# Half-position selective scans taken by pairs of states, with the side products of a lane moved

## The chip, the cores and the metric

The program runs on one core of one Trainium2 chip. The metric is the device time of one execution in microseconds. Each core has TensorE (PE, with its weight loads PEld), VectorE (DVE), ScalarE (ACT), GpSimd (POOL) and SyncE (SP, which here issues the DMAs); each of them works through its own instructions in order, and they meet at semaphores.

## The reference

Four images of 384 x 32 x 32 go through two layers. Layer 0: a scan in four directions (K0 = 4, 384 channels, 16 states) and a small FFN. Layer 1: a Mamba block (768 channels, 16 states) and a mixture of 4 experts. What the change touches is the recurrence, for each channel, direction and state n:

```
dA = exp(dt * A[n])
h  = h * dA + (dt * u) * B[n]
y += h * C[n]          # summed over the 16 states
```

with `dt = softplus(...)`, B and C rows shared by all channels of a direction. After it come the skip product, gates, output projections and norms.

## The kernel before

Channels lie on the 128 partitions, positions (1024 per image) on the free axis. The first image and its Mamba block take whole rows of 1024 (`lane_scans`, before 1237 us); the other three images and Mamba blocks take half rows of 512 (`fused_scans`), which is what the change touches. The program calls it three times for images (24 lanes each: 4 directions x 2 halves x 3 channel tiles) and three times for Mamba (12 lanes: 2 halves x 6 tiles). Lanes go half by half: the first half of a direction starts from zero and its last states are kept in `carry`, the second half starts from them.

A lane is 16 steps, one for each state. ACT's `decay(s)` writes exp(dt A) into a PSUM bank (L1297). POOL's `drive(s)` multiplies du by the B row (L1400, ring of DRIVES = 3). DVE's `scan(s)` runs the recurrence (L1449) and writes h over the decay, or into a `held` buffer where `by_pool(s)` holds. `weigh(s)` multiplies h by the C row: on DVE into `prods` for 11 states of a lane (L1458), on POOL in place in `held` for 5 (L1410). PE's `add(s)` sums over the states in bank 0 by four transposing matmuls (L1157). ACT copies that sum (`copy_sum`, L1321, step 3 of the next lane), PE turns it back (`back`, L1201), and a `take` on DVE (images) or `take_skipped` on ACT (Mamba) brings it to its place. In first halves, ACT's `keep` (L1289) and a POOL copy (L1408) save the last state before its bank or buffer is reused.

For the next lane, PE makes the dt product (L1141), ACT takes abs, exp and ln of it (L1277, L1281, L1285), DVE makes delta (L1430) and POOL du (L1389).

The order of each engine is written out by hand, by the constants `..._AT`: at which step of a lane an engine does what. Banks 1 to 4 of PSUM are a ring (SLOTS = 4): the list `places` names who takes the next one, steps and, between them, the projection of the next direction, delta, sum, output, gate input and residual. Whoever takes a place waits in `vacated` for the occupant four places earlier: a step weighed on DVE frees its bank with its weighing (and keep), one held for POOL with its scan.

Into this are woven guests: the expert products of the image before (`up`, `gelu`, `down` on banks 5 to 7). The gelus, a pair at a time with a table load ahead and one behind (L1341, L1379), stand behind the decay of steps 8, 13 and 18 (= 2 of the next lane) in images, 8 and 16 (= 0) in Mamba. Mamba lanes 0, 1, 2, 5, 6, 7 make a gate besides, with a silu and two table loads on ACT; lanes 8 to 10 an output product, lane 4 a projection; image lanes 0 to 7 turn a residual tile, lanes 1, 4, 7, 10, 13, 16, 19 project. In image lanes 0 to 2 ACT turns the image (L1363) at step 14.

## Time and profile before

| | |
|---|---|
| median of three runs | 5609.17 us (5603.15 to 5609.78) |
| the profiled execution's own time | 5607.85 us |
| its span | 5606.0 us, 73119 instructions, mean granted clock 0.945 |
| busy over the span | PE 86%, DVE 79%, POOL 71%, ACT 65% |
| half scans of images | about 1237 to 1930, 2555 to 3240, 3866 to 4550 us |
| half scans of Mamba | about 2100 to 2460, 3410 to 3760, 4700 to 5080 us |

Busy time is counted per engine. A wait is put down to the semaphore that came last. In a time line the difference of two starts on one engine is what an instruction costs its engine; it can be a little less than its length, since one overlaps the next.

### The profile page before, as it was taken

Reading aid. Unit: us, or ns where it says so; the run is one execution under the profiler, and the core shown is the slowest. Engines: PE = TensorE matmul, PEld = TensorE weight load, DVE = VectorE, ACT = ScalarE, POOL = GpSimd, SP = SyncE. Lnnn points to the kernel's source line nnn. Section 1 sums busy time; section 2 is a strip of 40 time slices with the busy share of each in tenths; the row PEclk is TensorE's granted clock in tenths of the full one; section 3 lists DMA queues with packets and bytes.
Section 4 is the critical chain, followed back from the end, with each engine's and each line's share of the span. In section 5 each row is a group of like instructions: output and inputs, shape, how many; then the busy total and the mean of one; then the engine's idle time right before and its main releaser. Section 6 shows DMA issues by size and latency. Waiting matters only on the chain. (4 is left out here: it accounts for less than half of the span.)

```text
span 5606.0 us, 73119 instructions
## 1 busy us (share of the span) xinstructions
PE 4828.6 (86%) x23205; PEld 3411.3 (61%) x23205; DVE 4445.6 (79%) x4529; ACT 3634.0 (65%) x5725; POOL 3960.4 (71%) x3074
## 2 busy tenths in 40 slices
PE   7888797789898887888989888888998988888998
PEld 5776546656666645555666645565666654556777
DVE  6889838959999848977999957996999975896544
ACT  5666455448887757767878857775878865775222
POOL 5888619839999818857999935894999962984111
PEclk9999999989999998998999999998999999999999
DMA  5777607737877616647788724654877842562110
GB/s 206 263 252 264 211 10 258 252 132 254 287 268 268 226 34 219 224 135 250 260 280 271 269 69 171 220 183 161 281 266 276 271 166 102 201 216 93 43 43 29
DMA packets 356676, 1104.83 MB, mean 197 GB/s; under 512 B 33210, under 2 KB 121126, under 8 KB 354872
## 3 DMA queue, kind: packets, MB, share of 16 engines
q1 hardware_dynamic: 356280, 1100.06, 56.9%
q8 instruction: 187, 3.06, 0.2%
q14 instruction: 209, 1.71, 0.1%
HBM read 1086.24 MB, written 13.68 MB: 196 GB/s over the span
## 5 line engine op out<-in xcount | busy, mean ns | idle before, releaser
L1157 PE MATMUL banks<-ident,prod 128*128 128x128 f32 x4752 | 764.9, 287 | 392.5 <-DVE prod L1458 286.6
L1157 PEld LDWEIGHTS banks<-ident,prod 128*128 128x128 f32 x4752 | 556.8, 145 | 799.1 <-DVE prod L1458 557.8
L1449 DVE TENSOR_TENSOR_SCAN banks<-banks,h 128x512 f32<-128x512 f32 x594 | 723.3, 1218 | 85.8 <-ACT banks L1297 48.5
L1400 POOL TENSOR_TENSOR h<-lane,Bb 128x512 f32<-128x512 f32 x576 | 722.8, 1272 | 57.8 <-DMA Bb<-half_rows 33.8
L1297 ACT ACTIVATE banks<-lane,A 128x512 f32<-128x512 f32 x864 | 581.1, 686 | 251.6 <-DVE prod L1458 82.4
L1229 PE MATMUL banks<-w_a,Cb 128*128 128x384 f32 x1536 | 552.2, 488 | 0.0
L1449 DVE TENSOR_TENSOR_SCAN banks<-banks,half_carry_a,h 128x512 f32<-128x512 f32 x396 | 505.5, 1277 | 8.8 <-ACT banks L1297 4.9
L1400 POOL TENSOR_TENSOR h<-half_du_a,Bb 128x512 f32<-128x512 f32 x384 | 482.7, 1275 | 14.8 <-DMA Bb<-half_rows 10.1
L1297 ACT ACTIVATE banks<-half_delta_a,A 128x512 f32<-128x512 f32 x576 | 385.3, 685 | 151.5 <-DVE lane L1430 73.7
L1217 PE MATMUL banks<-big,w_a 128*128 128x256 f32 x1728 | 435.0, 394 | 1.0 <-DMA w_a<-w_in 0.8
L1458 DVE TENSOR_TENSOR prod<-banks,half_C_a 128x512 f32<-128x512 f32 x528 | 365.3, 692 | 73.4 <-DMA half_C_a<-half_rows 2.4
L506 PE MATMUL banks<-diagonals_first,Cb 128*128 128x128 f32 x2304 | 318.1, 296 | 90.2 <-DVE h L771 39.0
L1400 POOL TENSOR_TENSOR h<-lane,Cb 128x512 f32<-128x512 f32 x288 | 362.7, 1272 | 24.8 <-DVE banks L1449 14.9
L659 ACT ACTIVATE banks<-delta_first,A 128x1024 f32<-128x1024 f32 x144 | 160.7, 1116 | 333.0 <-DVE prod L778 243.9
L506 PEld LDWEIGHTS banks<-diagonals_first,Cb 128*128 128x128 f32 x2304 | 299.7, 209 | 123.9 <-issue 120.4
L1341 ACT ACT_TABLE_LOAD x288 | 369.5, 1283 | 7.1 <-PE banks L1229 1.9
L1379 ACT ACT_TABLE_LOAD x288 | 369.5, 1283 | 5.2
L1217 PEld LDWEIGHTS banks<-big,w_a 128*128 128x128 f32 x1728 | 325.7, 198 | 61.7 <-issue 11.6
L1229 PEld LDWEIGHTS banks<-w_a,Cb 128*128 128x128 f32 x1536 | 269.7, 191 | 127.2 <-issue 12.0
L2436 POOL TENSOR_TENSOR w_lo<-raw,w_hi 128x1152 fp32r<-128x1152 f32 x32 | 89.3, 2812 | 352.8 <-ACT w_hi L2516 352.7
L1410 POOL TENSOR_TENSOR h<-h,half_C_a 128x512 f32<-128x512 f32 x240 | 305.0, 1271 | 46.6 <-DVE h L1449 36.0
L1157 PE MATMUL banks<-ident,h 128*128 128x128 f32 x2160 | 334.3, 279 | 0.0
(471 smaller groups left out, 12291.6 us busy)
## 6 DMA issues: line engine op xcount, KB each, us to landing
Bb<-half_rows SPq DMA_DIRECT2D x576, 512.0 KB, 4.3
C_first<-rows SPq DMA_DIRECT2D x288, 512.0 KB, 5.4
Cb<-half_rows SPq DMA_DIRECT2D x288, 512.0 KB, 4.4
w_a<-w_in SPq DMA_DIRECT2D x256, 576.0 KB, 6.1
w_b<-w_in SPq DMA_DIRECT2D x128, 576.0 KB, 6.2
half_C_a<-half_rows SPq DMA_DIRECT2D x128, 512.0 KB, 6.7
Bb<-rows SPq DMA_DIRECT2D x96, 512.0 KB, 5.5
half_C_b<-half_rows SPq DMA_DIRECT2D x64, 512.0 KB, 6.6
```

What stands on the lines that cost most here:

```text
L506: mm = eng.matmul(in_bank(2 + 2 * (s % SLOTS), k), m.du_turned[i % 2][:, block_of(k)], diagonal(n)[:, block_of(k)], start=k % (HALF // P) ...
L659: eng.activation(to, m.delta[:, i % 2, :], ACT.Exp, scale=lanes[i].A[:, a:a + 1]).then_inc(st.decay, 1)
L1157: mm = eng.matmul(ps[:, 0, at], src[:, at], m.ident[:, :], start=n == 0 and k == 0, stop=added(s) == (i + 1) * N, is_transpose=True, skip_ ...
L1217: mm = eng.matmul(hidden(u), g.w1[:, w % WRING, k, t * P:(t + 1) * P], g.un[:, k, at], start=k == 0, stop=k == CT - 1, skip_group_check=True)
L1229: mm = eng.matmul(total(b), g.h[:, u % HRING, b * P:(b + 1) * P], g.w2[:, w % WRING, t, :], start=u % PER == 0, stop=u % PER == PER - 1, s ...
L1297: eng.activation(slot(s), m.delta[i % 2], ACT.Exp, scale=x.A(j, n)).then_inc(st.decay, 1)
L1341: eng.activation(g.h[:, u % HRING, :], hidden(u), ACT.Gelu, bias=m.vec[:, b:b + 1]).then_inc(st.gelu, 1)
L1379: eng.preload_act_table_set(EXP_LN)
L1400: eng.tensor_tensor(m.dBu[:, s % DRIVES, :], m.du[i % 2], m.B[b % BRING][:, cols(s % 2)], ALU.mult).then_inc(st.dbu, 1)
L1410: eng.tensor_tensor(h, h, m.C[:, s % N, :], ALU.mult).then_inc(st.pooled, 1)
L1449: eng.tensor_tensor_scan(flip(to), flip(slot(s)), flip(m.dBu[:, s % DRIVES, :]), initial, ALU.mult, ALU.add).then_inc(st.scanned, 1)
L1458: eng.tensor_tensor(prods[own(s) % PRODS], slot(s), m.C[:, n, :], ALU.mult).then_inc(st.prod, 1)
```

## The change

Drives, weighings and keeps go by pairs of states (1024 wide instead of 512, one instruction where there were two); scans and decays stay one for each state. Of the eight pairs of a lane, 0, 3 and 5 are weighed on POOL and the others on DVE (6 and 10 states, where it was 5 and 11). The rings are of pairs: two drives, two products, two held (one of them in new SBUF). The bank ring keeps its four banks, but a pair takes two neighbouring ones, so that `places` is filled up with `None` behind or ahead of a lone side product; `vacated` skips a `None` to the occupant before it. Projection, residual, gate input and output product stand ahead of step 14, are made by PE at steps 12 and 13 and copied by ACT at step 15. The dt product goes from step 0 behind the add to step 1, ahead of adds; abs, exp, ln stand behind decay 4 (before: behind decay 5); du goes from step 14 to ahead of the drive of pair 4. PE makes adds after the side products of a step. POOL runs one drive ahead and weighs a pair after the drive of the second next. The two late silu inputs move to `prod[:, 2]`, and `turned_sum` too.

```diff
+def late_input(m, f):
+    return m.prod[:, CT - 1, cols(LATE_SILUS.index(f))]
...
-    SLOTS, DRIVES, PRODS, HELD, BRING = 4, 3, 3, 3, 3
+    SLOTS, DRIVES, PRODS, HELD, BRING = 4, 2, 2, 2, 3
-    PROJECT_AT, LOW_AT, STORE_AT = 11, 13, 15
-    COPY_AT, BACK_AT, TAKE_AT, SUM_AT, DELTA_AT = 3, 4, 7, 8, 4
-    SKIP_TAKE_AT = 9
-    BEHIND = 2
-    GATE_AT, PRODUCT_AT, OUT_AT, OUT_COPY_AT = 9, 6, 9, 11
+    ALL_PAIRS = LANES * PAIRS
+    POOLED, DU_AT, BEHIND = (0, 3, 5), 3, 2
+    DELTA_PLACE_AT, SUM_PLACE_AT, OTHER_PLACE_AT = 4, 8, 14
+    DT_AT, MAGNITUDE_AT, DELTA_AT = 1, 4, 5
+    COPY_AT, BACK_AT, TAKE_AT, SKIP_TAKE_AT, GATE_AT = 3, 6, 8, 9, 10
+    PROJECT_AT, LOW_AT, STORE_AT = 12, 15, 15
+    PRODUCT_AT, OUT_COPY_AT = 12, 15
-    INPUT_AT, INPUT_PLACE_AT, INPUT_TAKE_AT = 6, 9, 11
+    INPUT_AT, INPUT_TAKE_AT = 12, 15
-    TURN_AT, TURN_PLACE_AT, TURN_TAKE_AT = 11, 14, 15
+    TURN_AT, TURN_TAKE_AT = 12, 15
...
-        return s % N % 3 == 1
...
+    def by_pool(b):
+        return b % PAIRS in POOLED
...
-        if fresh(step // N + 2) and step % N == PROJECT_AT:
-            places.append(("projection", step // N + 2))
-        if step // N + 1 < LANES and step % N == DELTA_AT:
-            places.append(("delta", step // N + 1))
-        if step // N and step % N == SUM_AT:
-            places.append(("sum", step // N - 1))
-        if step // N in product_of and step % N == OUT_AT:
-            places.append(("out", product_of[step // N]))
-        if step // N in input_of and step % N == INPUT_PLACE_AT:
-            places.append(("input", input_of[step // N]))
-        if step // N in turned_of and step % N == TURN_PLACE_AT:
-            places.append(("residual", turned_of[step // N]))
+        i, n = step // N, step % N
+        if i + 1 < LANES and n == DELTA_PLACE_AT:
+            places.extend((None, ("delta", i + 1)))
+        if i and n == SUM_PLACE_AT:
+            together(("sum", i - 1))
+        if n == OTHER_PLACE_AT:
+            together(*([("projection", i + 2)] if fresh(i + 2) else []),
+                     *([("out", product_of[i])] if i in product_of else []),
+                     *([("input", input_of[i])] if i in input_of else []),
+                     *([("residual", turned_of[i])] if i in turned_of else []))
...
+    def slots(b):
+        first, second = (1 + place_of["step", s] % SLOTS for s in (2 * b, 2 * b + 1))
+        assert second == first + 1
+        return ps[:, first:first + 2, :]
...
+        at = place_of[what, k] - SLOTS
+        while at >= 0 and places[at] is None:
+            at -= SLOTS
+        if at < 0:
...
+        before, b = places[at]
...
+                for r in range(2):
+                    for k in range(HALF // P):
+                        at = slice(k * P, (k + 1) * P)
+                        mm = eng.matmul(ps[:, 0, at], src[:, r, at], m.ident[:, :], start=first and r == 0 and k == 0,
+                                        stop=r == 1 and added(b) == (i + 1) * PAIRS, is_transpose=True, skip_group_check=True)
...
                 if s in ups and n == 0:
                     up(ups[s])
                 if s < STEPS:
-                    if not by_pool(s):
-                        add(s)
-                    if n >= BEHIND and by_pool(s - BEHIND):
-                        add(s - BEHIND)
                     if i and n == BACK_AT:
                         back(i - 1)
                     if i in product_of and n in (PRODUCT_AT, PRODUCT_AT + 1):
                         product(product_of[i], n - PRODUCT_AT)
                     if i in input_of and n == INPUT_AT:
                         gate_product(input_of[i])
-                    if fresh(i + 2) and n in (PROJECT_AT - 3, PROJECT_AT - 2):
-                        project(i + 2, n - PROJECT_AT + 3)
-                    if i + 1 < LANES and n == DELTA_AT - 4:
+                    if fresh(i + 2) and n in (PROJECT_AT, PROJECT_AT + 1):
+                        project(i + 2, n - PROJECT_AT)
+                    if i + 1 < LANES and n == DT_AT:
                         dt_product(i + 1)
                     if i in turned_of and n == TURN_AT:
                         turn_residual(turned_of[i])
+                    if n % 2:
+                        if not by_pool(s // 2):
+                            add(s // 2)
+                        if n // 2 >= BEHIND and by_pool(s // 2 - BEHIND):
+                            add(s // 2 - BEHIND)
...
-                    if i + 1 < LANES and n == DELTA_AT + 1:
+                    if i + 1 < LANES and n == MAGNITUDE_AT:
...
-                if s >= DRIVES:
-                    eng.wait_ge(st.scanned, s - DRIVES + 1)
-                eng.tensor_tensor(m.dBu[:, s % DRIVES, :], m.du[i % 2], m.B[b % BRING][:, cols(s % 2)],
-                                  ALU.mult).then_inc(st.dbu, 1)
...
+                if b >= DRIVES:
+                    eng.wait_ge(st.scanned, 2 * (b - DRIVES + 1))
+                eng.tensor_tensor(drives[b % DRIVES], over_tiles(m.du[i % 2], 2),
+                                  m.B[b % BRING].rearrange("p (r l) -> p r l", r=2), ALU.mult).then_inc(st.dbu, 1)
...
+                eng.tensor_tensor(h, h, m.C[:, 2 * q:2 * q + 2, :], ALU.mult).then_inc(st.pooled, 1)
...
-            for s in range(STEPS):
-                i, n = s // N, s % N
-                drive(s)
-                if n >= BEHIND and by_pool(s - BEHIND):
-                    weigh(s - BEHIND)
-                if n == 14 and i + 1 < LANES:
+            drive(0)
+            for b in range(ALL_PAIRS):
+                i, q = b // PAIRS, b % PAIRS
+                if q == DU_AT and i + 1 < LANES:
+                if b + 1 < ALL_PAIRS:
+                    drive(b + 1)
+                if q and by_pool(b - 1):
+                    weigh(b - 1)
...
-                eng.tensor_tensor(prods[own(s) % PRODS], slot(s), m.C[:, n, :], ALU.mult).then_inc(st.prod, 1)
...
+                eng.tensor_tensor(prods[own(b) % PRODS], slots(b), m.C[:, 2 * q:2 * q + 2, :], ALU.mult).then_inc(st.prod, 1)
...
+                    if n % 2 and not by_pool(s // 2):
+                        weigh(s // 2)
...
-        return m.prod[:, f % 3, cols(c)]
+        return late_input(m, f) if c and f in LATE_SILUS else m.prod[:, f % 3, cols(c)]
...
+                             drives=[two(m.h[:, 0, :]), two(m.h[:, 1, :])], held=[two(m.h[:, 2, :]), named_more],
+                             prods=[two(m.prod[:, 0, :]), two(m.prod[:, 1, :])], turned_sum=m.prod[:, 2, cols(0)], **named)
```

## Rows read from the trace of the kernel before

**Rows 1.** Busy time by stretch: length, then busy us of PE, PEld, DVE, ACT, POOL.

```profile
1320.25:1917.29 597.04, 539.25 (x2662) 380.55 (x2661) 560.49 (x600) 480.75 (x757) 552.43 (x487) 0.98 0.78 271
2135.08:2439.42 304.34, 258.27 (x1190) 174.60 (x1189) 278.07 (x292) 229.36 (x376) 276.86 (x248) 0.94 0.62 209
```

**Rows 2.** Waits of DVE, 1320 to 1917 us: who, for whom, us, times, longest.

```profile
DVE banks L1449 <- ACT banks L1297: 3.3, 9, 0.7
```

**Rows 3.** Time line of DVE, second half: start, length, engine, line, operation.

```profile
1516.11 0.68 DVE L1430 SCALAR_TENSOR_TENSOR lane<-banks,lane 128x512 f32<-128x512 f32 x1
1516.71 1.28 DVE L1449 TENSOR_TENSOR_SCAN banks<-banks,half_carry_a,h 128x512 f32<-128x512 f32 x1
1518.12 0.69 DVE L1458 TENSOR_TENSOR prod<-banks,half_C_a 128x512 f32<-128x512 f32 x1
1518.73 1.27 DVE L1449 TENSOR_TENSOR_SCAN h<-banks,half_carry_a,h 128x512 f32<-128x512 f32 x1
1519.92 0.66 DVE L2940 TENSOR_TENSOR big<-big,banks 128x512 f32<-128x512 f32 x1
```

**Rows 4.** Time line of POOL: `du` starts, 20 image lanes apart, then 10 Mamba lanes.

```profile
1320.25 1.28 POOL L1389 TENSOR_TENSOR half_du_a<-half_delta_a,big 128x512 f32<-128x512 f32 x1
...
1917.29 1.28 POOL L1389 TENSOR_TENSOR half_du_a<-half_delta_a,big 128x512 f32<-128x512 f32 x1
...
2135.08 1.27 POOL L1389 TENSOR_TENSOR half_du_a<-half_delta_a,big 128x512 f32<-128x512 f32 x1
...
2439.42 1.27 POOL L1389 TENSOR_TENSOR half_du_a<-half_delta_a,big 128x512 f32<-128x512 f32 x1
```

**Rows 5.** By source line, whole-position products of 128x1024: ns, least, median, most.

```profile
L778 DVE TENSOR_TENSOR prod<-banks,C_first x108: 1224/1225/1226, 60.3 to 1139.1; 128x1024 f32<-128x1024 f32 x108
L726 POOL TENSOR_TENSOR h<-du_first,Bb x48: 2338/2361/3152, 48.8 to 1121.0; 128x1024 f32<-128x1024 f32 x48
```

**Rows 6.** Time line of POOL in a first half: copy, weighing, drive.

```profile
1603.86 0.20 POOL L1408 COPY half_carry_a<-h 128x1 f32<-128x1 f32 x1
1604.14 1.27 POOL L1410 TENSOR_TENSOR h<-h,half_C_a 128x512 f32<-128x512 f32 x1
1605.37 1.27 POOL L1400 TENSOR_TENSOR h<-lane,Bb 128x512 f32<-128x512 f32 x1
```

**Rows 7.** Time line: weighing to decay with a keep between, decays to a scan.

```profile
1800.84 0.69 DVE L1458 TENSOR_TENSOR prod<-banks,half_C_a 128x512 f32<-128x512 f32 x1 [0.48 <-DVE banks L1449]
...
1801.83 0.69 ACT L1297 ACTIVATE banks<-half_delta_a,A 128x512 f32<-128x512 f32 x1
...
1641.04 1.30 ACT L1297 ACTIVATE banks<-half_delta_a,A 128x512 f32<-128x512 f32 x2
...
1641.77 1.23 DVE L1449 TENSOR_TENSOR_SCAN banks<-banks,h 128x512 f32<-128x512 f32 x1 [0.41 <-ACT banks L1297]
```

**Rows 8.** Time line of ACT: decays around gelus, then around abs, exp, ln.

```profile
2166.66 0.69 ACT L1297 ACTIVATE banks<-lane,A 128x512 f32<-128x512 f32 x1
...
2169.52 1.28 ACT L1379 ACT_TABLE_LOAD   x1
2170.82 0.69 ACT L1297 ACTIVATE banks<-lane,A 128x512 f32<-128x512 f32 x1
...
1511.00 0.69 ACT L1297 ACTIVATE banks<-half_delta_a,A 128x512 f32<-128x512 f32 x1 [1.24 <-DVE prod L1458]
...
1513.44 0.67 ACT L1297 ACTIVATE banks<-half_delta_a,A 128x512 f32<-128x512 f32 x1
```

**Rows 9.** Time line of ACT in Mamba: a gate's silu between two decays.

```profile
2159.49 0.69 ACT L1297 ACTIVATE banks<-half_delta_a,A 128x512 f32<-128x512 f32 x1
...
2163.40 0.69 ACT L1297 ACTIVATE banks<-half_delta_a,A 128x512 f32<-128x512 f32 x1
```

**Rows 10.** Groups of lines, ACT: the copy that turns the image.

```profile
L1363 ACT ACTIVATE big<-big 128x1024 f32<-128x1024 f32 x3 | 6.1, 2024 | 0.0
```

**Rows 11.** Waits of the whole trace: a scan for its decay.

```profile
DVE banks L1449 <- ACT banks L1297: 55.9, 76, 2.3
```

164 lines of the change are left out of this document (78 added, 86 removed).

## The prediction

> **What bounds the kernel now.** I read the busy times by stretch first: in two stretches inside the half-position scans, one with three pairs of guest units per lane and one with two, DVE is busy 94% and 91% of the time, POOL 93% and 91%, PE 90% and 85%, ACT 81% and 75% [rows 1]. So DVE and POOL share the bound and any loss of ACT's lead can add a third. Next the waits of DVE: in 597 us of the image stretch its scans waited 3.3 us for their decays [rows 2]. The rest of its idle time is inside its own order: a weigh starts 1.41 us after the scan that it reads, the next scan 0.61 us after a weigh, and a scan follows a scan that it doesn't depend on after 1.19 us [rows 3]. A lane of 16 states with a carried start is then 11 own states x (1.41 + 0.61) + 5 pooled x 1.19 = 28.2 us, plus 0.60 for delta and 0.58 for the take (0.66 long, less the overlap of 0.08 that the others have) [rows 3], 29.4 us. The starts of `du` measure lanes: 20 lanes in 1917.29 - 1320.25 = 597.0 us, 29.85 us each; 10 in 2439.42 - 2135.08 = 304.3 us, 30.4 us each [rows 4]. The sum and the measurement meet, so DVE's order is the bound, with ACT far enough ahead. Images run 3 x 23 such lane intervals (69), Mamba stages 3 x 11 (33). All else of the program is untouched.
>
> **Part 1, weighing by pairs (DVE).** Own states go from 11 of 16 to 10, and ten products of 512 become five of 1024. No half scan shows a product of 128x1024 on DVE; the same operation in the whole-position scans, PSUM bank times SBUF rows, takes 1.225 us [rows 5] against 0.69 [rows 3]. Instructions overlap the next by 0.08 us [rows 3], so an own pair is 1.19 + 1.41 + 1.145 = 3.74 us where it was 4.04, a pooled pair 2.38. A lane: 5 x 3.74 + 3 x 2.38 + 1.18 = 27.0 us: 2.4 us less than 29.4, if nothing waits.
>
> **Part 2, drives and weighing by pairs (POOL).** A 128x512 product starts every 1.23 us [rows 6]; a 128x1024 one takes 2.36 us in the whole scans [rows 5], about 2.34 from start to start. A lane had 21 x 1.23 + 1.23 for `du` = 27.1 us and gets 8 drives + 3 weighings = 11 x 2.34 + 1.23 = 27.0, plus in first halves 3 copies at 0.28 [rows 6] where there were 5. POOL stays level. The drive now reads du twice through a stride of zero, which the trace doesn't show: bounds 2.34 (contiguous) and 2.50 (two drives of 512, 2 x 1.23 + 0.04); I take the first, as the operand rows stay contiguous, and keep the other for a rival. A drive may only start when both scans of the pair before the last are done.
>
> **Part 3, banks.** This decides it. Before, four single banks let ACT write decays up to four states ahead. Now a pair holds two neighbouring banks from its decays to its weighing, so there are two places. Every guest of the ring (delta ahead of step 4, sum ahead of 8, projection/residual/gate/output ahead of 14) takes a whole place, and then the next pair reuses the place of the pair just ahead of it. From the `places` list: steps 4, 5 take the banks of steps 2, 3 (own: after their weighing); 8, 9 those of 6, 7 (pooled: after each scan); 14, 15 those of 12, 13 (own) in lanes with such a product at step 14; else pairs alternate. Prices: a decay takes 0.69, and a scan that waits for it starts 0.04 behind its end [rows 7]; I take 0.04 for a decay behind a weighing too. That makes 0.77 after the weighing's end; against a scan that would have started 0.08 before the weighing ended, this is 0.86 us. With a `keep` between, the decay starts 0.30 behind the end instead of 0.04, 0.26 more [rows 7]. Decay to decay is 1.30 - 0.69 = 0.61 [rows 7], but 4.16 with a pair of gelus between (two table loads, two activations) [rows 8], 2.44 with abs, exp, ln between [rows 8], 3.91 with a gate's silu [rows 9]. The gelus keep their steps (8, 13, 18 = 2 of the next lane in images; 8 and 16 = 0 in Mamba), and `MAGNITUDE_AT` is 4, between decays 4 and 5.
>
> Walk of a second-half image lane, scan 0 at 0 and decays 0, 1 ready:
> - Scan 2 at 2.38. Decay 2 starts at 0.11 (after the last lane's weighing), the gelus follow, decay 3 runs 4.27 to 4.96, scan 3 at 5.02 where DVE was free at 3.57: stall 1.45.
> - Weighing of pair 1 from 6.42 to 7.65. Decay 4 at 7.68, scan 4 at 8.43 (free at 7.57): 0.86. Decay 5 stands behind abs, exp, ln: 10.12 to 10.81, scan 5 at 10.87 (free at 9.62): 1.25.
> - Weighing 12.27, delta 13.41, scan 6 at 14.01, scan 7 at 15.20. `du` waits for delta, so the drive of pair 4 ends at 17.73. Decay 8 starts when scan 6 ends, 15.30, the gelus, decay 9 from 19.46 to 20.15. Scan 8 at 17.8, take, scan 9 at 20.21 (free at 18.16): 2.05.
> - Then 21.61 weighing 4, scans 10 to 13 at 22.76 to 26.33, weighing 6 at 27.73, scan 14 at 28.88 with decay 14 ready at 28.33 (the third gelus are hidden), weighing 7 at 31.47, next scan 0 at 32.62.
> So 27.0 + 5.6 = 32.6 us against 29.85: 2.8 more. A first half has scans shorter by 0.05 to 0.06 (1.23 long against 1.28, [rows 7, 3]) and longer keeps; the same walk gives 32.6, and POOL's drives of pairs 0, 1 and 6 come some 0.1 to 0.2 late: 32.7.
>
> **Part 4, the moved products.** Where something stands ahead of step 14, scan 14 stalls 0.86 (with keep 1.12). That is so in image lanes 0 to 7, 10, 13, 16, 19, twelve of 24: 12 us. In lanes 0 to 2 the copy that turns the image, 2.02 us [rows 10], now stands between two decays with no lead: 3 x 1.5 = 4.5. On PE dt_product waits for scan 1 only; behind it is the pair of guest up products, not due on DVE, so its place ahead of the adds costs nothing. SP's row store moves from the end of step 13's copy to 15; the rows are wanted a lane later. Ups at 7 wait for the gelus at 8; adds behind them are due only two own pairs later. PE's cover for these is its 10% idle.
> In Mamba the walk gives per lane 27.0 - 0.58 (no take) + stalls 0.1 + 0.86 + 1.25 + 2.63 (no take covers scan 9) = 31.25, +0.3 for gates: 31.55 against 30.4, 1.15 x 11 = 12.6. In four lanes (4, 8, 9, 10) a projection or output adds 0.86 + 1.05, since its copy and then the gelus at step 0 both stand ahead of the next decay 1: 7.6. In six lanes (0, 1, 2, 5, 6, 7) the silu of 3.91 is there: decay 14 at the end of weighing 6 (call it 0), decay 15 at 0.6, decay 0 at 4.6 (scan 0: stall 0.83), gelus, decay 1 from 8.76 to 9.45 (scan 1: 2.97); with scan 14's 0.86 this is 4.7 x 6 = 28.
>
> **The sum.** Image: 23 x 2.8 = 64.4, + 12 + 4.5, - 4 (lane 0 has no sum ahead of step 8, the last lane no delta) = 77, x 3 = 231. Mamba: 12.6 + 7.6 + 28.2 - 2.5 = 46, x 3 = 138. Together 369 us over the profiled execution's 5607.85 = 5977, of which the median of the runs is 1.3 away. I say 5975.
>
> **A rule beside a row.** The rows show the decay 1.30 us after the start of the table load ahead of it, and 4.16 - 0.61 = 3.55 us for the whole gelu block [rows 8]. The Trainium skill, page "ScalarE: Activation LUTs", section "What ACT_TABLE_LOAD costs", gives 1283 ns for the load, which agrees, and a drain of about 1380 ns besides on each switch. With it two switches would add 2.8 us to each gelu block, and with two exposed blocks in an image lane this would be 5.5 us a lane and some 380 us more over the images. These rows show no such drain, and I leave it out.
>
> **Rivals.**
> - *Decays are never late* (I misread the places, or the waits are released sooner). Then DVE's 27.0 (26.1 in first halves) and POOL's 27.0 (27.8) meet near 27.5: (29.85 - 27.5) x 69 + (30.4 - 27.5) x 33 = 258 us less, 5350. For it: in the trace DVE hardly waits for ACT. Against: there ACT has four single banks. It decides from the point at which decay 4 ends before weighing 1 does. This ends faster: 0.10.
> - *Only the stall at steps 4 and 5 stays, the gelus are hidden.* Image lanes are then 27.0 + 2.1 + 0.5 + 0.2 = 29.8, Mamba about 29.3: 0 x 69 - 1.1 x 33 = -36, 5570. For it: gelu blocks stood between decays before too and cost DVE little. Against: the cover between scan 6's end and scan 9 is two scans and a take, 3.0 us, for a chain of 4.16 + 0.69 = 4.9. 0.07, split between faster and same.
> - *POOL's drives cost more*, 2.50 by the two-drive bound and worse by the stride: the drives of pairs 4, 6 and 0 come later each lane, 0.5 to 1.0 us x 102 = 50 to 100 us: 6050. For it: POOL has only 5 us of slack in 32.6. 0.12.
> - *One of the three stall places is smaller than walked*, by 1.0 to 1.5 us a lane: 5830 to 5870. 0.08.
> My forecast has 0.63, 5900 to 6040.
>
> **How the numbers follow.** About 0.2% (11 us) is what a measurement of this kernel can tell from no change. Slower: 0.63 + 0.12 + 0.08 = 0.83; less a little for what I haven't thought of, 0.82. Faster 0.14, same 0.04. The range holds the forecast, the costlier drives and the smaller stall: 5820 to 6080, some 0.8.
>
> **What would show it.** DVE's waits for ACT at the scan should grow from 56 us in the whole trace [rows 11] to over 400; busy shares in the image stretch should fall for DVE from 94% to about 80%, and for POOL to about 82%. In the time line of a lane, scans 4, 5, 3 and 9 should stand after gaps of 0.9, 1.3, 1.5 and 2 us, and `du` should start every 32.7 to 33.7 us. The DVE product should be 1.225 us and POOL's 2.36 (part 1 and 2 right). If lanes are 27.5 us, part 3 is wrong; if POOL is over 90% busy and the drives release the scans, the third rival holds.

## Result and the profile after

The changed kernel takes 6148.23 us (median of four runs, 6145.56 to 6159.04), the kernel before 5606.16 (four runs): 1.0973 times the time before, with a 95% interval of 1.0955 to 1.0991. That is 542 us slower. I had forecast slower, at 5975, in a range up to 6080: the direction was right, the size was 369 us instead of 542, and the measured time lies 68 us above the range.

The work itself shrank as meant: 69276 instructions instead of 73119, and DVE is busy for 4335.1 us instead of 4445.6. The busy shares of the page of after fell on every engine: everything waits more. In microseconds only PE got busier, 4971.5 instead of 4828.6 for the same 23205 matmuls; its mean granted clock was 0.916, before 0.945.

```profile
PE 4971.5 (81%) x23205; PEld 3554.5 (58%) x23205; DVE 4335.1 (71%) x3881; ACT 3597.1 (59%) x5401; POOL 3898.8 (63%) x1886
```

The groups of the page of after say that the instructions by pairs have the lengths that the whole scans showed [rows 5]: 1225 ns on DVE, about 2356 on POOL (busy us, mean ns of one, idle time before them and who ended it).

```profile
L1420 POOL TENSOR_TENSOR h<-lane,Bb 128x1024 f32<-128x1024 f32 x288 | 676.7, 2355 | 147.1 <-DVE h L1472 132.9
...
L1481 DVE TENSOR_TENSOR prod<-banks,half_C_a 128x1024 f32<-128x1024 f32 x240 | 294.0, 1225 | 31.8
```

The stretches that answer to rows 1, 650 us within the images and the ten Mamba lanes (length, then busy us of PE, PEld, DVE, ACT, POOL, the granted clock, DMA share, GB/s):

```profile
1308.66:1958.84 650.18, 541.43 (x2553) 388.38 (x2551) 516.80 (x461) 455.58 (x676) 516.46 (x258) 0.93 0.69 243
2213.79:2594.14 380.35, 280.63 (x1191) 197.59 (x1190) 270.80 (x233) 229.78 (x352) 270.79 (x137) 0.85 0.52 177
```

In images DVE is now busy 79% (516.80 / 650.18), and POOL as much; in Mamba both 71%. Before it was 94 and 91% for DVE. The granted clock in the Mamba stretch is 0.85 where it was 0.94 [rows 1]. The waits of DVE over the whole trace (us, times, longest) answer to rows 2 and 11, where a scan waited 55.9 us for its decay:

```profile
DVE banks L1472 <- ACT banks L1318: 443.5, 421, 2.3
...
DVE banks L1472 <- POOL h L1420: 84.9, 60, 1.6
DVE half_more_a L1472 <- ACT banks L1318: 77.1, 26, 5.9
DVE h L1472 <- ACT banks L1318: 73.7, 24, 5.8
```

With `half_more_b` (39.0) the scans wait 633 us for decays. The starts of `du` measure the lanes, as in rows 4, here the first and the last of each stretch:

```profile
1243.54 1.27 POOL L1410 TENSOR_TENSOR half_du_a<-half_delta_a,big 128x512 f32<-128x512 f32 x1 [1.56 <-DVE half_delta_a L1452]
...
1991.57 1.27 POOL L1410 TENSOR_TENSOR half_du_a<-half_delta_a,big 128x512 f32<-128x512 f32 x1 [4.59 <-DVE half_delta_a L1452]
...
2213.79 1.27 POOL L1410 TENSOR_TENSOR half_du_a<-half_delta_a,big 128x512 f32<-128x512 f32 x1 [2.95 <-DVE half_delta_a L1452]
...
2594.14 1.28 POOL L1410 TENSOR_TENSOR half_du_a<-half_delta_a,big 128x512 f32<-128x512 f32 x1 [3.12 <-DVE half_delta_a L1452]
```

22 image lanes take 748.0 us; the same 22 took 659.15 before (+88.9 a stage). Ten Mamba lanes (0 to 9) take 380.35 instead of 304.3 [rows 4] (+76.0). The one Mamba lane among them without a projection, gate input or output product, lane 3, takes 32.75; the gate lanes 0, 1, 2, 5, 6, 7 take 37.2 to 38.2; lanes 4, 8 and 9, with a projection or an output product, take 41.0, 39.8 and 40.8.

**A plain image lane, as it runs.** The time line of DVE at the end of the first image stage (start, length, operation; in brackets the idle time before it and who ended it; neighbouring instructions are joined; the first row is scans 6 and 7, the second scan 8):

```profile
1958.84 2.45 DVE L1472 TENSOR_TENSOR_SCAN h<-banks,half_carry_a,h 128x512 f32<-128x512 f32 x2
1962.67 1.29 DVE L1472 TENSOR_TENSOR_SCAN banks<-banks,half_carry_a,h 128x512 f32<-128x512 f32 x1 [1.38 <-issue]
...
1979.78 1.27 DVE L1472 TENSOR_TENSOR_SCAN banks<-banks,half_carry_a,h 128x512 f32<-128x512 f32 x1
1982.41 1.29 DVE L1472 TENSOR_TENSOR_SCAN banks<-banks,half_carry_a,h 128x512 f32<-128x512 f32 x1 [1.36 <-ACT banks L1318]
1983.84 1.23 DVE L1481 TENSOR_TENSOR prod<-banks,half_C_a 128x1024 f32<-128x1024 f32 x1
1985.82 1.29 DVE L1472 TENSOR_TENSOR_SCAN banks<-banks,half_carry_a,h 128x512 f32<-128x512 f32 x1 [0.76 <-ACT banks L1318]
1988.24 1.29 DVE L1472 TENSOR_TENSOR_SCAN banks<-banks,half_carry_a,h 128x512 f32<-128x512 f32 x1 [1.13 <-ACT banks L1318]
```

The rows from 1979.78 on are scans 2, 3, the weighing of pair 1, scans 4 and 5 of the next lane. The walk had stalls of 1.45, 0.86 and 1.25 us there, counted from where DVE would have started by overlap; the idle times shown are shorter by that overlap of some 0.1. Why decay 4 is late stands in the time line of ACT one lane earlier:

```profile
1949.76 0.58 ACT L1342 ACTIVATE prod<-banks 128x512 f32<-128x512 f32 x1
...
1951.28 1.22 DVE L1481 TENSOR_TENSOR prod<-banks,half_C_a 128x1024 f32<-128x1024 f32 x1
1952.54 0.69 ACT L1318 ACTIVATE banks<-half_delta_a,A 128x512 f32<-128x512 f32 x1 [2.20 <-DVE prod L1481]
```

ACT has nothing to do for 2.20 us and then starts 0.04 behind the end of the weighing: the pair that is weighed holds the only place. Scan 8 starts 3.83 behind scan 6 (1962.67 - 1958.84), held up by the drive of pair 4; the walk had 3.79. Behind the take scan 9 then waits another 0.49 us for its decay.

**A Mamba lane with an output product, lane 8, at its end:**

```profile
2522.23 1.12 PE L1177 MATMUL banks<-ident,prod 128*128 128x128 f32 x8 [4.43 <-DVE prod L1481]
2523.16 4.44 PE L1237 MATMUL banks<-late_un,w_a 128*128 128x256 f32 x12
...
2529.61 2.74 PE L1188 MATMUL banks<-big,w_out_a 128*128 128x512 f32 x6
2532.18 1.45 PE L1249 MATMUL banks<-w_a,Cb 128*128 128x384 f32 x4
2533.47 2.74 PE L1188 MATMUL banks<-big,w_out_a 128*128 128x512 f32 x6
2536.25 0.60 ACT L1322 ACTIVATE big<-banks 128x512 f32<-128x512 f32 x1 [6.66 <-PE banks L1188]
...
2537.67 1.28 DVE L1472 TENSOR_TENSOR_SCAN half_more_a<-banks,half_carry_a,h 128x512 f32<-128x512 f32 x1 [4.83 <-ACT banks L1318]
...
2541.82 1.28 DVE L1472 TENSOR_TENSOR_SCAN half_more_a<-banks,half_carry_a,h 128x512 f32<-128x512 f32 x1 [2.87 <-ACT banks L1318]
```

The two halves of the product, with a `down` between, end at 2536.21. ACT had waited 6.66 us with its copy, and behind the copy stand decay 0, the gelus and decay 1. So scan 0 is 4.83 late, scan 1 another 2.87.

The chain on PE begins earlier than the product. PE idles 4.43 us until DVE has weighed pair 4, and from 2522.23 on it works without a gap: the add, twelve `up` matmuls, an add, a `down`, and then the three pieces named. The `up` matmuls take 4.44 us; twelve of them took 2.75 in the kernel before. The granted clock differs (the matmuls before, then a stretch of each kernel: length, the busy us of the engines, the clock, DMA share and GB/s):

```profile
2377.32 2.75 PE L1217 MATMUL banks<-late_un,w_a 128*128 128x256 f32 x12
...
2376.00:2381.00 5.00, 5.00 (x32) 4.36 (x30) 4.73 (x6) 3.37 (x6) 4.33 (x5) 1.00 0.41 133
...
2524.00:2526.00 2.00, 2.00 (x6) 1.64 (x5) 2.00 (x3) 0.00 (x0) 1.32 (x2) 0.50 0.46 178
```

The first two rows are of the kernel before, at the full clock of 2.4 GHz; the last is of the changed one, at half of it, behind the idle time. So about 1.7 us of this chain goes with the lower clock; no run holds the clock fixed. The product itself ran at 1.00 (2530 to 2536).

### The profile page after: what moved, and what is told of

Its sections match the earlier page's. It is cut to its first block and busy times, and to the rows that moved or that the text cites. A ratio compares the mean times of both kernels' runs of the same rounds, so it can differ in the third digit from the quotient of the medians.

```text
span 6145.4 us, 69276 instructions
## 1 busy us (share of the span) xinstructions
PE 4971.5 (81%) x23205; PEld 3554.5 (58%) x23205; DVE 4335.1 (71%) x3881; ACT 3597.1 (59%) x5401; POOL 3898.8 (63%) x1886
## 5 line engine op out<-in xcount | busy, mean ns | idle before, releaser
L1177 PE MATMUL banks<-ident,prod 128*128 128x128 f32 x4320 | 661.5, 304 | 666.6 <-DVE prod L1481 664.3
L1472 DVE TENSOR_TENSOR_SCAN banks<-banks,h 128x512 f32<-128x512 f32 x540 | 648.6, 1221 | 334.1 <-ACT banks L1318 247.3
L1420 POOL TENSOR_TENSOR h<-lane,Bb 128x1024 f32<-128x1024 f32 x288 | 676.7, 2355 | 147.1 <-DVE h L1472 132.9
L1249 PE MATMUL banks<-w_a,Cb 128*128 128x384 f32 x1536 | 575.1, 507 | 0.0
L1472 DVE TENSOR_TENSOR_SCAN banks<-banks,half_carry_a,h 128x512 f32<-128x512 f32 x360 | 452.3, 1279 | 170.8 <-ACT banks L1318 130.7
L1420 POOL TENSOR_TENSOR h<-half_du_a,Bb 128x1024 f32<-128x1024 f32 x192 | 451.6, 2357 | 110.1 <-DVE half_more_a L1472 96.2
L1420 POOL TENSOR_TENSOR h<-lane,Cb 128x1024 f32<-128x1024 f32 x144 | 339.3, 2356 | 63.4 <-DVE h L1472 43.6
L1249 PEld LDWEIGHTS banks<-w_a,Cb 128*128 128x128 f32 x1536 | 290.4, 202 | 145.5 <-issue 30.4
L1481 DVE TENSOR_TENSOR prod<-banks,half_C_a 128x1024 f32<-128x1024 f32 x240 | 294.0, 1225 | 31.8
L529 PE MATMUL banks<-ident,prod 128*128 128x128 f32 x1584 | 214.4, 283 | 92.1 <-DVE prod L783 91.6
L1249 PE MATMUL banks<-w_b,Cb 128*128 128x384 f32 x768 | 286.8, 506 | 0.0
```

The lines of the kernel that those rows point to most:

```text
L529: mm = eng.matmul(in_bank(0, k), src[:, block_of(k)], m.ident[:, :], start=s == first_add[i] and k % (HALF // P) == 0, stop=place[s] == al ...
L1177: mm = eng.matmul(ps[:, 0, at], src[:, r, at], m.ident[:, :], start=first and r == 0 and k == 0, stop=r == 1 and added(b) == (i + 1) * PAI ...
L1249: mm = eng.matmul(total(b), g.h[:, u % HRING, b * P:(b + 1) * P], g.w2[:, w % WRING, t, :], start=u % PER == 0, stop=u % PER == PER - 1, s ...
L1420: eng.tensor_tensor(drives[b % DRIVES], over_tiles(m.du[i % 2], 2), m.B[b % BRING].rearrange("p (r l) -> p r l", r=2), ALU.mult).then_inc( ...
L1472: eng.tensor_tensor_scan(flip(to), flip(slot(s)), flip(drives[b % DRIVES][:, r, :]), initial, ALU.mult, ALU.add).then_inc(st.scanned, 1)
L1481: eng.tensor_tensor(prods[own(b) % PRODS], slots(b), m.C[:, 2 * q:2 * q + 2, :], ALU.mult).then_inc(st.prod, 1)
```

## The experiments

All are medians in us, of two runs unless said otherwise; a ratio is to the kernel before, timed beside it (medians of 5603 to 5612), with its 95% interval. Unless said otherwise a kernel differs from the changed one by the lines shown.

### One cause at a time

**abs, exp and ln one step earlier (e1_mag3).**

```diff
-    DT_AT, MAGNITUDE_AT, DELTA_AT = 1, 4, 5
+    DT_AT, MAGNITUDE_AT, DELTA_AT = 1, 3, 5
```

> The changed kernel with abs, exp and ln behind decay 3 instead of decay 4 (MAGNITUDE_AT = 3), nothing else. Theory A (ACT has lost its lead because a pair and every side product take two of the four banks): decay 5 no longer stands behind 1.83 us of other work, the 1.2 us gap ahead of scan 5 goes in all 102 lane intervals, 120 us less, about 6030. Theory B (POOL's drives by pairs pace the lane, the ACT waits only stand where a POOL wait would otherwise stand): under 30 us less, about 6130.

Measured 6011.58, ratio 1.0722 (1.069 to 1.0754): 137 less than the change. Plain second-half image lanes take 31.3 to 31.4. The stall of scan 5 is what the walk said; it goes when ACT does this in its own waiting time.

**Gelus one step later (e2_gelus_later).**

```diff
-                        ... guests, ((0, 8, 11), (9, 16, 19)),
+                        ... guests, ((0, 9, 11), (9, 17, 19)),
...
-                                ((2, 8, 9), (7, 13, 14), (12, 18, 21)), ...
+                                ((2, 9, 9), (7, 13, 14), (12, 19, 21)), ...
```

> The changed kernel with the exposed gelu pairs one step later: behind decay 9 instead of 8 and behind decay 3 instead of 2 in images, 9 instead of 8 and 1 instead of 0 in Mamba, so that both decays of a pair stand ahead of the 3.55 us block. Theory A: in an image lane the stall at scan 3 (1.4 us) goes and that around scans 8 and 9 shrinks by 0.7 to 1.0; in Mamba 1 to 2 us a lane: 150 to 220 us less, 5930 to 6000. Theory B: under 30 us.

Measured 6029.97, ratio 1.0755 (1.0706 to 1.0804): 118 less, short of what I expected. Plain lanes fell to 30.8 to 31.0.

**Pair 0 weighed on DVE, pair 1 on POOL (e3_pooled_135).**

```diff
-    POOLED, DU_AT, BEHIND = (0, 3, 5), 3, 2
+    POOLED, DU_AT, BEHIND = (1, 3, 5), 3, 2
```

> The changed kernel with pair 1 instead of pair 0 weighed on POOL (pairs 1, 3, 5), so that steps 4 and 5 reuse banks that are free with the scans 2 and 3, and scan 3 has the weighing of pair 0 ahead of it. The work of each engine stays the same. Theory A: the 0.86 us at scan 4 goes, that at scan 5 shrinks by 0.3, that at scan 3 goes in images: 2.6 us an image lane and 1.2 a Mamba lane, some 220 us less, 5930. Theory B: no change in POOL's work, so under 30 us.

Measured 5921.22, ratio 1.0561 (1.0529 to 1.0592): 227 less. Plain second-half image lanes take 30.25. The amount of work on each engine is the same; only the place that steps 4 and 5 inherit is no longer freed by a weighing, but by the scans themselves, and scan 3 has the weighing of pair 0 ahead of it.

**No table loads (e4_no_table).** The guests' Gelu is left out (Identity stands in its place) and the two loads around each pair go.

> The changed kernel where the guests' gelu in the half scans is an identity with bias, with no table load ahead or behind: the gelu itself and two table loads of 1.28 us are left out, the activations of 0.47 us stay. It measures what the table loads cost a ring without lead. Theory A: the block between two decays falls from 3.55 to 1.0 us, image lanes lose 2.4 us, Mamba lanes 3 to 4: some 280 us less, 5870, of a work that is 370 us of ACT's busy time twice. Theory B: ACT is only 59% busy and gives back little, under 60 us.

Measured 5889.2, ratio 1.0504 (1.0461 to 1.0546): 259 less. The gelu block, 3.55 us [rows 8], is what makes scans 3 and 9 late.

The time lines say which stalls went. Below is the idle time of DVE ahead of its scans in one plain lane, lane 21 of the first image stage (- is none over 0.2 us); the length is from its scan 0 to the next lane's:

| kernel | length | scan 3 | scan 4 | scan 5 | scan 8 | scan 9 |
|---|---|---|---|---|---|---|
| changed | 32.50 | 1.30 | 0.76 | 1.13 | 1.38 | 0.49 |
| e1_mag3 | 31.27 | 1.30 | 0.76 | - | 1.39 | 0.48 |
| e2_gelus_later | 30.79 | - | 0.76 | 1.13 | 1.39 | - |
| e3_pooled_135 | 30.19 | - | - | 1.05 | 1.39 | 0.48 |
| e4_no_table | 30.79 | - | 0.76 | 1.12 | 1.39 | - |

So the terms of the image walk are each borne out one at a time, and in this lane leaving the gelus out is worth no more than moving them a step. The savings don't add, as the combined runs below show.

**The output product cut short (e7_short_product).**

```diff
-                for k in range(half * CT, (half + 1) * CT):
+                for k in (half * (TILES - 1),):
```

> The changed kernel where each half of the output product in Mamba lanes 8 to 10 is one matmul instead of three (four of six matmuls of 0.43 us left out, nothing else). Theory A (ACT's copy, and behind it decay 0, waits for PE's chain): each of the nine lanes is 1.7 us shorter, up to 15 us less in all, and the wait of ACT for this product falls by 1.7 us each. Theory B (it waits for something else that is late at the same time): no change.

Measured 6117.13, ratio 1.0903 (1.0871 to 1.0935): 31 less. Lane 8 fell from 39.83 to 36.39, lane 9 from 40.81 to 37.39, so each of the nine lanes got 3.4 shorter. The difference to what I expected is PE's price: six instructions of the product's first half take 2.74 us (above), 0.86 for a matmul, which runs as two instructions. I had counted one.

### The moved side products by themselves

**In the kernel before, only the side products moved (e6_before_sides).** Its states stay single and its four banks too; abs, exp and ln stand behind decay 4 as well.

```diff
-    PROJECT_AT, LOW_AT, STORE_AT = 11, 13, 15
+    PROJECT_AT, LOW_AT, STORE_AT = 14, 15, 15
-    GATE_AT, PRODUCT_AT, OUT_AT, OUT_COPY_AT = 9, 6, 9, 11
+    GATE_AT, PRODUCT_AT, OUT_AT, OUT_COPY_AT = 9, 12, 14, 15
-    INPUT_AT, INPUT_PLACE_AT, INPUT_TAKE_AT = 6, 9, 11
+    INPUT_AT, INPUT_PLACE_AT, INPUT_TAKE_AT = 12, 14, 15
-    TURN_AT, TURN_PLACE_AT, TURN_TAKE_AT = 11, 14, 15
+    TURN_AT, TURN_PLACE_AT, TURN_TAKE_AT = 12, 14, 15
```

> The kernel before with only the moved side products of the change: places ahead of step 14, PE at steps 12 and 13, ACT's copies at 15, and abs, exp, ln behind decay 4; single states, single banks. Theory A (it is the pairs' two places that turn these steps into stalls): 0 to 50 us more, 5605 to 5655, the most of it in Mamba where a gate's table loads and a gelu block now follow each other. Theory C (the moved products cost by themselves, pairs or not): 150 us more or worse.

Measured 5860.99, ratio 1.0446 (1.0416 to 1.0477): 250 slower than the kernel before, and I had expected nearly nothing. The waits of this kernel:

```profile
DVE banks L1449 <- ACT banks L1297: 246.0, 149, 7.6
...
ACT big L1301 <- PE banks L1168: 80.8, 9, 9.2
```

The second row is the copy of the output product: nine waits of 9.0 us, where the kernel before had nine of 1.0 (9.2 in all). In the changed kernel they sum to 66.0. So four single banks don't help: the copy stands in ACT's order, and every decay behind it waits. Image lanes got 22.6 us a stage longer (681.7 for 22), ten Mamba lanes 55.7 (360.0).

**abs, exp and ln behind decay 4 alone, in the kernel before (e11_before_mag4).**

```diff
-                    if i + 1 < LANES and n == DELTA_AT + 1:
+                    if i + 1 < LANES and n == DELTA_AT:
```

> The kernel before with abs, exp, ln behind decay 4 instead of 5, nothing else. It splits the run with moved side products, which had this too. Both theories: within 15 us of the kernel before, since four single banks keep ACT ahead; if it is more than 50 us slower, that part belongs to this step and not to the side products.

Measured 5628.53 (eight runs), ratio 1.0039 (1.0026 to 1.0053): 21 slower. The side products' own share of e6 is therefore about 250 - 21 = 230 us.

**The same move taken back in the changed kernel, by two steps (e5_sides_10) and by four (e9_sides_8).** Shown is e9; e5 has 12, 10 and 13 in place of 10, 8 and 11.

```diff
-    DELTA_PLACE_AT, SUM_PLACE_AT, OTHER_PLACE_AT = 4, 8, 14
+    DELTA_PLACE_AT, SUM_PLACE_AT, OTHER_PLACE_AT = 4, 8, 10
-    PROJECT_AT, LOW_AT, STORE_AT = 12, 15, 15
-    PRODUCT_AT, OUT_COPY_AT = 12, 15
+    PROJECT_AT, LOW_AT, STORE_AT = 8, 11, 15
+    PRODUCT_AT, OUT_COPY_AT = 8, 11
-    INPUT_AT, INPUT_TAKE_AT = 12, 15
+    INPUT_AT, INPUT_TAKE_AT = 8, 11
-    TURN_AT, TURN_TAKE_AT = 12, 15
+    TURN_AT, TURN_TAKE_AT = 8, 11
```

> The changed kernel with projection, residual, gate input and output product two steps earlier: their place ahead of step 12, PE at steps 10 and 11, ACT's copy at 13. Their place then follows pair 5, whose banks are free with its scans, and the copy no longer stands between decay 15 and the next lane's decay 0. Theory A (lead lost at the ring, and in Mamba PE's chain of product, guest product, product in front of the copy): the 0.86 us at scan 14 goes in all such lanes, and Mamba lane intervals with an output product or projection fall from 40 to 41 us to about 33, with a gate from 37.5 to about 33; together some 220 us less, 5930. Theory B (the Mamba excess is the later step of the stores and C loads behind it, not these products): under 60 us.

e5 measured 6174.87, ratio 1.1006 (1.0974 to 1.1038): 27 above the change, which the intervals can't tell from none, where I had expected 220 less. Ten Mamba lanes did fall, from 380.35 to 358.9, but the images lost 34 us a stage. Its time line shows what the copy at 13 meets there:

```profile
1627.57 2.77 PE L1149 MATMUL banks<-big,w0x 128*44 128x512 f32 x6
1630.38 0.59 ACT L1292 ACTIVATE lane<-banks 44x512 f32<-44x512 f32 x1 [2.09 <-PE banks L1149]
1630.99 1.28 ACT L1362 ACT_TABLE_LOAD   x1
...
1635.16 2.47 DVE L1472 TENSOR_TENSOR_SCAN banks<-banks,half_carry_a,h 128x512 f32<-128x512 f32 x2 [3.88 <-ACT banks L1318]
```

The copy waits 2.09 us for PE, the gelus of step 13 stand directly behind it, and the decays behind those: DVE waits 3.88.

> The changed kernel with the side products near where they were: place ahead of step 10, PE at 8 and 9, ACT's copy at 11, clear of the gelus at 8, 13 and 16 and of the end of the lane; nothing else. Theory A2 (half of the loss is the side products' own chain: PE's product behind guest products, then ACT's copy, then a gelu block, all ahead of the next decays; the other half is the two places of the pairs): Mamba intervals fall from 37 to 41 us to about 33, image lanes with one stay (0.86 us moves from scan 14 to scan 10): 110 to 150 us less, 6000 to 6040. Theory B2 (in the pair ring any place for them costs the same): no change.

e9 measured 6057.75, ratio 1.079 (1.0758 to 1.0821): 90 less than the change, 20 short of what I expected. The Mamba lanes with a side product fell to 33.7 to 36.3 from 37.2 to 41.0, while 22 image lanes took 761.4, 13 more than in the change, where I had expected none.

### Repairs together

**All four at once (e8_all)**: MAGNITUDE_AT 3, gelus later, POOLED (1, 3, 5), side products at 10 and 13.

> The changed kernel with all four repairs: abs, exp, ln behind decay 3, the exposed gelus one step later, pairs 1, 3, 5 on POOL, the side products at steps 10 and 11. Pairs stay. Theory A: no reuse of a pair's banks right behind itself is left that ACT can't cover; lanes come to 28.5 to 29.5 us, set by DVE's 27.0 and by POOL's drive of pair 4 behind du: 5500 to 5600, level with or below the kernel before. Theory D (pairs cost by their grain, two buffers instead of three or four, whatever the steps): above 5700.

Measured 6154.8, ratio 1.0970 (1.0938 to 1.1002): no gain at all over the change. Each of the first three alone had brought 118 to 227. The time line:

```profile
1816.91 0.60 ACT L1298 ACTIVATE half_du_a<-banks 128x512 f32<-128x512 f32 x1 [2.35 <-PE banks L1159]
...
1823.02 2.47 DVE L1472 TENSOR_TENSOR_SCAN banks<-banks,half_carry_a,h 128x512 f32<-128x512 f32 x2 [5.02 <-ACT banks L1318]
```

The dt product takes the bank of step 1. With pair 0 on DVE that bank is free only with the weighing of pair 0; in the changed kernel it is free with scan 1. So PE starts the dt product behind the weighing, abs at step 3 waits 2.35 us for it, and then come exp, ln and the gelus of step 3, all ahead of decay 4.

**Repairs that don't meet.** e10_repaired has POOLED (1, 3, 5), MAGNITUDE_AT 3, the gelus of step 8 behind decay 9 in images and Mamba, and the side products at 8 and 11. e12_three_repairs is e10 with the side products where the change has them.

> The changed kernel with pairs 1, 3, 5 on POOL, abs, exp, ln behind decay 3, the gelus of step 8 behind decay 9, and the side products at 8, 9, 11; the gelus of 18 and 16 stay, since pair 0 is now weighed on DVE and covers them. Theory A2: every named stall but one (0.86 us behind a side product) is gone; image lanes come to 29 to 30 us, Mamba to 31 to 32: 5560 to 5700. Theory D (the grain of pairs costs by itself): above 5750.

> As the repaired kernel, but with the side products at steps 12, 13 and 15 as the change has them. What is between this run and that one is the price of their place in a ring that is otherwise mended. Theory A2: 120 to 180 us slower than the repaired one, about 5720. Theory B2: the same as the repaired one.

e10 measured 5830.28, ratio 1.0384 (1.0354 to 1.0415), 130 over the range of theory A2 and on the side of theory D; e12 5967.47, ratio 1.0629 (1.0598 to 1.066). The difference of 137 is the price of the moved side products once the rest is mended, as expected. But e12 is slower than e3 alone (5921.22), and its time line shows the early abs waiting for the same dt product:

```profile
1717.72 1.09 PE L1159 MATMUL banks<-lane,lowk 13*128 13x512 f32 x2 [0.91 <-DVE prod L1481]
1719.06 0.59 ACT L1298 ACTIVATE lane<-banks 128x512 f32<-128x512 f32 x1
...
1721.58 2.47 DVE L1472 TENSOR_TENSOR_SCAN banks<-banks,half_carry_a,h 128x512 f32<-128x512 f32 x2 [1.63 <-ACT banks L1318]
```

So I moved it to the other side: **e13_pool_mag5** is POOLED (1, 3, 5), MAGNITUDE_AT 5, side products at 8 and 11, gelus as in the change; **e14_gelu9** is e13 with the same gelus behind decay 9 as in e10; **e15_du4** is e14 with DU_AT 4; **e16_du4_alone** is the changed kernel with nothing but DU_AT 4.

```diff
-    POOLED, DU_AT, BEHIND = (0, 3, 5), 3, 2
+    POOLED, DU_AT, BEHIND = (1, 3, 5), 4, 2
-    DT_AT, MAGNITUDE_AT, DELTA_AT = 1, 4, 5
+    DT_AT, MAGNITUDE_AT, DELTA_AT = 1, 5, 5
```

> The changed kernel with pairs 1, 3, 5 on POOL, side products at 8, 9, 11, and abs, exp, ln behind decay 5. The repaired kernel had them behind decay 3, where they waited for a dt product that itself waits for pair 0's weighing, and held up decay 4. Theory A2: 0.9 to 1.6 us a lane less than that, 5700 to 5740. Theory D (pairs cost by their grain): as the repaired kernel, 5830.

> The one before with the gelus of step 8 behind decay 9. Theory A2: scan 9 no longer waits, scan 8 still waits for POOL's drive of pair 4: 0.6 us a lane less, 5640 to 5680. Theory D: the same as the one before.

> The one before with du ahead of the drive of pair 5 instead of pair 4 (DU_AT = 4), so that the drive of pair 4 doesn't stand behind a du that waits for delta. Theory A2: the 1.4 us at scan 8 goes, lanes come near DVE's own 27 to 28.5 us: 5520 to 5580, below the kernel before. Theory D: no lower than 5650, since POOL has 27 us of work in a lane too and two buffers can't hide what is left.

> The changed kernel with DU_AT = 4 alone. In its lanes scan 8 waits 1.4 us for the drive behind du, but scan 9 would wait as long for decay 9 behind the gelus anyway. Theory A2: the wait only changes its name, 0 to 20 us less. Theory B: POOL's drives pace the lane, 100 us less or more.

e13 measured 5732.09, ratio 1.0217 (1.0187 to 1.0246), as expected; e14 5686.14, ratio 1.0135 (1.0105 to 1.0164), 46 less; e15 5629.65 (eight runs), ratio 1.0041 (1.0029 to 1.0053), 56 less again; e16 6149.57, ratio 1.0961 (1.0929 to 1.0993), no change. e14 differs from e10 only in the step of abs, exp and ln, 5 instead of 3: that is worth 144 us, and e14 lies within the range that theory A2 had set for e10. In e16, lane 21 has no stall at scan 8 any more and 1.98 us at scan 9, so the wait did change its name. `du` one pair later is worth nothing while ACT is late, and 56 us once it isn't. e15 is the best version by pairs, and it is still 23 us behind the kernel before; that is between theory A2 (5520 to 5580) and theory D (no lower than 5650), and neither holds as I put it.

### Why the best one isn't faster

DVE's own work in a plain lane is 27.0 us by the sum of the prediction, yet plain lanes of e15 take 29.2 to 29.7. In the middle of one of them, POOL and DVE:

```profile
1877.27 1.28 POOL L1410 TENSOR_TENSOR lane<-lane,big 128x512 f32<-128x512 f32 x1
...
1878.50 2.38 POOL L1420 TENSOR_TENSOR h<-half_du_a,Cb 128x1024 f32<-128x1024 f32 x1
...
1880.82 2.39 POOL L1430 TENSOR_TENSOR h<-h,half_C_a 128x1024 f32<-128x1024 f32 x1
...
1883.13 4.70 POOL L1420 TENSOR_TENSOR h<-half_du_a,Bb 128x1024 f32<-128x1024 f32 x2
...
1885.60 2.47 DVE L1472 TENSOR_TENSOR_SCAN banks<-banks,half_carry_a,h 128x512 f32<-128x512 f32 x2 [1.36 <-issue]
```

The trace names no releaser for the 1.36 us, but scan 12 starts at 1885.60, and the first of the two drives, of pair 6, ends near 1883.13 + 2.36 = 1885.49. It stands behind `du`, a drive and a weighing. Two more kernels take them out of its way: e17_du7 has DU_AT 7, and e18_weigh_later also weighs pair 5 behind the next lane's first drive.

```diff
-                if q and by_pool(b - 1):
+                if q and q != PAIRS - 2 and by_pool(b - 1):
                     weigh(b - 1)
+                if q == PAIRS - 1 and by_pool(b - 2):
+                    weigh(b - 2)
```

> As the kernel with DU_AT 4, but DU_AT 7: GpSimd makes du of the next lane ahead of the drive of that lane's pair 0, not ahead of the drive of pair 5. In the trace of DU_AT 4 a plain image lane is 29.2 to 29.7 us; its DVE work is 27.0, and its largest gap is 1.36 us ahead of scan 12, which starts when the drive of pair 6 ends. That drive stands behind du (1.28), the drive of pair 5 and the weighing of pair 3. Theory A (GpSimd's order holds the lane): scan 12 waits no more, but with du there the drive of the next pair 0 ends some 0.8 late, so 0.5 us a lane is won, 35 us in all over 69 image lanes: 5580 to 5605. Theory B (ScalarE's order holds it: decays 12 and 13 end just as late as the drive): no change, 5615 to 5640. Mamba lanes wait 2.07 us for decay 12 there and shouldn't move under either.

> As the run before it (DU_AT 7), and GpSimd weighs pair 5 behind the drive of the next lane's pair 0, not ahead of it. Theory A (GpSimd's order): the drive of pair 0 then ends some 1.4 us ahead of the scan that wants it, and both gaps go, 1.3 to 1.8 us a lane in images: 90 to 120 us less than with DU_AT 4, 5510 to 5545, which would be the first version by pairs that is faster than the kernel before (5606). Theory B (ScalarE): no change, 5610 to 5640. Rival C: the later weighing of pair 5 holds up PE's add and the take behind it, which eats some 0.5 us a lane: 5545 to 5580.

e17 measured 5650.8 (six runs), ratio 1.0064 (1.0052 to 1.0076); e18 5644.06 (five runs), ratio 1.0055 (1.0042 to 1.0068). Neither theory holds as I put it. By the ratios e17 is some 13 us and e18 some 8 us slower than e15, and the interval of e18 overlaps that of e15, so it can't be told from no change. The gap was POOL's doing: ahead of scan 12 of lane 21 it went from 1.36 us to 0.37 and 0.35, and the shortest image lanes fell from 29.15 to 28.81 and 28.23 us (before: 29.28). But other waits came: in e17 lane 21 has 1.60 us ahead of scan 0, for a drive, and 1.01 ahead of scan 8, for a decay; in e18 one lane of 29.41 became 32.75. In e18 a drive then waits for its B rows (the transfer), and a scan for the drive:

```profile
1889.75 2.35 POOL L1420 TENSOR_TENSOR h<-half_du_a,Bb 128x1024 f32<-128x1024 f32 x1 [1.77 <-DMA Bb<-half_rows]
...
1892.19 1.29 DVE L1474 TENSOR_TENSOR_SCAN banks<-banks,half_carry_a,h 128x512 f32<-128x512 f32 x1 [3.98 <-issue]
```

Over its trace POOL's drives wait 87.4 us for B rows, in e15 15.3. In e17 it is 20.4, and its scans wait 145.0 us for drives where e15 has 105.8. That the rows are what a shorter lane meets next is seen in the trace of e18 only; whether more buffers for them would bring the pairs below the kernel before wasn't tried.

## Why the prediction was right in kind and short in size

**Parts 1 and 2, weighing and drives by pairs: right.** 1.225 and 2.355 us measured; the stride of zero costs nothing, so the third rival (POOL's drives cost more) falls.

**Part 3, the banks: the walk was right, to a tenth in plain lanes; what it was compared with was not.** The plain second-half lane was walked at 32.62 us and takes 32.55 to 32.70. The stalls stand where the walk put them, and e1, e3 and e4 take them away one by one (137, 227 and 259 us). The rival with no late decay (5350) and the one with stalls at steps 4 and 5 only (5570) fall with that, and so does the one with a smaller stall. But the 29.85 us that I set against the walk holds work that the walk lacks, the sums of the guests' expert outputs on DVE (below). The rule that I left out, a drain of about 1380 ns at each table switch (the Trainium skill, page "ScalarE: Activation LUTs", section "What ACT_TABLE_LOAD costs"), isn't in this trace either: decay to load, load to gelus and load to decay follow at 0.71, 1.29 and 1.29 us (1944.98, 1945.69, 1946.98 for the first three starts of a block in the change, 1947.84 and 1949.13 for the last two).

**Part 4, the moved products: this is the step that failed.** Its words were "PE's cover for these is its 10% idle", and a price of "0.86 + 1.05" (1.9 us) in Mamba lanes with a projection or output. I counted ACT's copy and the bank, and not that the copy comes at the end of a chain on PE: `up` matmuls (4.4 us in lane 8 at the lower clock, 1.7 more than at the full one), half a product of 2.6 us, a `down` of 1.3, half a product of 2.6, issued only at steps 12 and 13, with the copy due at 15, and decay 0, gelus and decay 1 all behind it. Lanes 4, 8 and 9 take 40.56 on the mean, where I had 31.55 + 1.9 = 33.45: 7.1 too little in each. In gate lanes I had 36.25 and they take 37.65 on the mean: 1.4 short. The trace shows two causes: in 12 of the 18 ACT waits for the gate's product of PE (13.9 us together, at most 2.0), and DVE's own gate product, in lanes 1 to 6, takes 1.62 us of its order in five and 1.20 in the sixth, where I had counted 0.3 a lane on the mean. Lane 3, which has that gate product too, is 1.2 short. Together 3 x 7.1 + 6 x 1.4 + 1.2 = 31 us of the ten lanes, 93 for three stages. It isn't only a matter of the ring: the same moves without any pairs cost 230 us (e6 less e11), and 137 once the pairs are otherwise mended (e12 less e10).

**The sum.** Images gave 88.9 a stage instead of 77 (of 23 lanes), 36 us more over three. This is not what stands at step 14. In ten of the 22 lane intervals of the first stage DVE also adds up a guest's expert output, which the walk left out; here between scans 8 and 9 of a lane with nothing at step 14:

```profile
1526.60 1.23 DVE L1472 TENSOR_TENSOR_SCAN banks<-banks,h 128x512 f32<-128x512 f32 x1 [1.51 <-POOL h L1420]
...
1529.00 1.14 DVE L1508 SCALAR_TENSOR_TENSOR xt_a<-banks,weights,xt_a 128x384 f32<-128x384 f32 x2 [0.59 <-PE banks L1249]
1530.06 1.22 DVE L1472 TENSOR_TENSOR_SCAN banks<-banks,h 128x512 f32<-128x512 f32 x1
```

Scan 9 starts 3.46 behind scan 8, where the walk has 2.41. Those ten intervals are together 11.7 us longer than the walk with its prices for step 14 gives. Of the twelve others ten agree with it within 0.11 us, the first and the fourth are 0.7 and 0.4 longer. The kernel before has the same sums: of the 20 intervals behind the 29.85 us the ten without one take 29.44 on the mean, the ten with one 30.26. So my 29.4 was the lane without, I took its distance to 29.85 for agreement, and 3 x 23 lanes were set some 0.4 us too low. No experiment isolates this term.

With the Mamba lanes' 93 this is 129 of the 173 us that were missing. The other 44 us lie outside these intervals, at the joints of the stages. From the last `du` of an image stage to the first of Mamba it is 4.4 us more than before, from there to the next image stage 12.5 more; the last lane of each stage, which the sum did count, is in these. I didn't follow them instruction by instruction, so that part stays open.

**The signs that I named.** Waits for ACT over 400: 443.5 at the banks alone. DVE at about 80% in images: 79%. POOL about 82%: 79%. `du` every 32.7 to 33.7 us: plain lanes without a guest's sum take 32.6 to 32.7, the others 32.9 to 36.0. The gaps of scans 3, 4 and 5: there. The 2 us at scan 9 are two waits, 1.38 at scan 8 for the drive of pair 4 and 0.49 at scan 9 for its decay.

## What to carry to other kernels

Taking two units at once halves the number of places in a ring of fixed size, and what goes is the producer's lead; count the lead first, in places, at every step at which a guest takes one. A side product's cost is not its own time but what stands behind its copy: follow it from the product's first matmul to the consumer's next input, in the order of each engine, and look where on that order a table load or another copy stands. When a walk of the new order is set against a measured lane of the old one, both must hold the same work. Repairs of a hand-made order don't add; measure them together, and expect the next engine (here POOL's order, then the transfers of rows) to take over what the first one gives back.
